# Feed-forward rows normalised inside the attention before it, and a projection that alternates between two banks

## The reference

```
x = x + tanh(g_xattn[0]) * window_attention(layernorm(x), ctx)      # 8 heads, window 16
x = x + tanh(g_ffn[0])   * quantised_ffn(layernorm(x))
x = x + tanh(g_xattn[1]) * lane_attention(layernorm(x), ctx, ctx)   # 4 lanes, mixed by a matrix
x = x + tanh(g_ffn[1])   * lora_swiglu(layernorm(x))

lora_swiglu(x): gate = x Wg' + (x Ag') Bg';  up = x Wu' + (x Au') Bu'
                h = silu(gate) * up;         out = h Wd' + (h Ad') Bd'
```

## Time and profile before

| what | value |
| --- | --- |
| median of 3 runs | 3566.77 us |
| all runs | 3562.18, 3566.77, 3567.2 us |
| the profiled execution | 3563.57 us, of which the span is 3561.9 us |
| PE busy in the span | 3269.9 us (92%) |
| DVE, ACT, POOL busy | 1429.4, 888.1, 348.5 us |
| blocks' first DMA at | w 0.80, f 413.39, kv 893.07, a 1333.90, l 1985.97, g 2004.87 us |

### The profile page before, as it was taken

How to read it: one execution, slowest core, us unless ns; L and a number is a source line. 1 busy time by engine, 2 the same in 40 slices (tenths; PEclk the granted TensorE clock), 3 DMA queues, 4 the chain that set the end, 5 groups by cost and what they waited for, 6 DMA issues and landing times. The chain is left out here.

```text
span 3561.9 us, 52640 instructions
## 1 busy us (share of the span) xinstructions
PE 3269.9 (92%) x21076; PEld 2512.2 (71%) x21076; DVE 1429.4 (40%) x2021; ACT 888.1 (25%) x1232; POOL 348.5 (10%) x304
## 2 busy tenths in 40 slices
PE   6999658998799996999999389999999999999999
PEld 3555545777688874666666378888888888778777
DVE  7787568882200006776776351122212211310000
ACT  2233243342211114554554121111111111200000
POOL 2000000000000002322322111111111110000000
PEclk9999779999699998999999699999999999999999
DMA  5666432221322213111211432222222222643443
GB/s 112 137 144 143 124 110 72 75 69 45 122 64 71 71 54 118 70 78 59 88 59 47 130 109 90 96 96 90 89 96 96 94 86 84 223 149 116 142 141 103
DMA packets 339441, 352.61 MB, mean 99 GB/s; under 512 B 154352, under 2 KB 261472, under 8 KB 337264
## 3 DMA queue, kind: packets, MB, share of 16 engines
q1 hardware_dynamic: 339312, 350.79, 31.6%
HBM read 215.23 MB, written 126.97 MB: 96 GB/s over the span
## 5 line engine op out<-in xcount | busy, mean ns | idle before, releaser
L2230 PE MATMUL g_ps<-g_xs,g_wt 128*128 128x512 f32 x4128 | 957.9, 392 | 0.0
L2230 PEld LDWEIGHTS g_ps<-g_xs,g_wt 128*128 128x128 f32 x4128 | 774.8, 189 | 160.8
L2286 PE MATMUL g_ps<-g_wd,g_h 128*128 128x512 f32 x2016 | 463.8, 392 | 6.4 <-DMA g_h<-g_hidden 3.3
L2286 PEld LDWEIGHTS g_ps<-g_wd,g_h 128*128 128x128 f32 x2016 | 380.9, 189 | 88.5 <-DMA g_h<-g_hidden 5.0
L2148 DVE SCALAR_TENSOR_TENSOR g_act_out<-g_ps,g_g,g_act_out 128x512 f32<-128x512 f32 (+1 forms) x88 | 66.0, 750 | 691.2 <-ACT g_act_out L2080 691.2
L2080 ACT ACTIVATE g_act_out<-g_ps 128x512 f32<-128x512 f32 (+1 forms) x88 | 52.6, 598 | 655.3 <-PE g_ps L2230 655.2
L1280 PE MATMUL kv_gps<-kv_xh,kv_wh 128*128 128x512 f32 x512 | 200.8, 392 | 0.0
L1280 PE MATMUL kv_gps<-kv_xl,kv_wh 128*128 128x512 f32 x512 | 199.4, 389 | 0.0
L1280 PE MATMUL kv_gps<-kv_xh,kv_wl 128*128 128x512 f32 x512 | 199.2, 389 | 0.0
L1025 PE MATMUL f_gps<-f_xt,f_qwh 128*128 128x256 f32 x1024 | 193.9, 290 | 1.4 <-DVE f_xt L903 1.4
L1628 PEld LDWEIGHTS a_tps<-a_ident,a_e 128*128 128x128 f32 x1024 | 112.1, 143 | 104.9 <-issue 91.2
(11 more groups left out here) (247 smaller groups left out, 4381.2 us busy)
## 6 DMA issues: line engine op xcount, KB each, us to landing
g_h<-g_hidden SPq DMA_DIRECT2D x176, 256.0 KB, 2.7
g_hidden<-g_h SPq DMA_DIRECT2D x84, 512.0 KB, 2.7
kv<-kv_y SPq DMA_DIRECT2D x16, 1024.0 KB, 5.7
a_kv<-kv SPq DMA_DIRECT2D x16, 1024.0 KB, 4.8
g_xb<-x SPq DMA_DIRECT2D x24, 512.0 KB, 4.1
g_down<-g_raw SPq DMA_DIRECT2D x22, 512.0 KB, 2.8
g_raw<-g_down SPq DMA_DIRECT2D x22, 512.0 KB, 4.1
g_raw<-in_L_ffn_gate_w_dram SPq DMA_DIRECT2D x21, 512.0 KB, 4.0
```

Source lines behind the costliest of these rows:

```text
L2230: w = pe.matmul(gps[:, c % 2, m, :], wt[m][i][:, l, ks], xs[c][:, r, k, :], start=(k == 0 and a == 0), stop=(k == NK - 1 and a == 2))
L2286: w = pe.matmul(to, tile[:, p % RING, l, cols], wd[f][:, r, os], start=(f == 0 and a == 0), stop=False)
```

## The change

- Window attention: the second half of the queries and of the values goes into the bank of the ring that the next batch's first or second scores will use (`half_bank`); x has five slots instead of four and is loaded one batch further ahead.
- `lora_stacks` is gone as a block. Its six loads and 18 stores stand on ACT's own DMA queue in `projections`, its two instructions on ACT and DVE there.
- Lane attention also normalises its finished rows: in event W, ahead of the addition of batch b-1, DVE and POOL normalise y of batch b-2 into `a_yn`, and SP stores it to `x3n`. The last batch is normalised after the last addition. The first pass of the loop is written out.
- Feed-forward loads these rows. Tiles 0 to 11 have eight slots `g_xa` in a part of memory that group 3 fills later; 12 to 15 use `g_xb`. Tiles 0 to 7 alternate between two pairs of banks. The first product waits for the gate's weights only, not for the up weights.

```diff
 window_attention
+        def half_bank(n, i, a):
+            return prj[:, :] if a == 0 or i == 1 else sps[:, (NK * n + i // 2) % RING, :]
 project
-                    pe.wait_ge(S["sbk"], 2 * n + 2) if a == 0 else pe.wait_ge(S["sbq"], 2 * n + 1)
+                    pe.wait_ge(S["sbk"], 2 * n + 2) if a == 0 else past(pe, "sel", NK * n - RING + 1)
 values
-                pe.wait_ge(S["sbq"], 2 * n + 2) if a == 0 else pe.wait_ge(S["sbv"], 2 * n + 1)
+                pe.wait_ge(S["sbq"], 2 * n + 1) if a == 0 else past(pe, "sel", NK * n - RING + 2)
 scores
+                if t == 1:
+                    pe.wait_ge(S["sbv"], 2 * n + 2)
...
 projections, ACT
+            for (a, _, _), at, width in zip(jobs, starts, widths):
+                act.dma_start(factors[:, at:at + width], flat(a)).then_inc(S["factors"], 16)
...
             weights(1, 1)
+            act.wait_ge(S["factors"], 16 * len(jobs))
+            act.copy(parts[:, 0, :], factors[:, :]).then_inc(S["high"], 1)
             results(0, 0)
+            act.wait_ge(S["low"], 1)
...
...
 lane_attention, POOL (end of a pass)
+                if not isinstance(b, int) or b >= 2:
+                    power(b - 2)
 lane_attention, DVE
+            def norm_rows(n):
+                layer_norm_steps(nc, dve, S, n, y, st, mv, S["rstd"])
+                dve.wait_ge(S["ynout"], 16 * n)
+                dve.tensor_scalar(yn[:, :], y[:, :], mv[:, 0:1], rstd[:, 0:1], ALU.subtract, ALU.mult).then_inc(S["yn"], 1)
                     elif ev == "W":
+                        if not isinstance(b, int) or b >= 2:
+                            norm_rows(b - 2)
+                            dve.wait_ge(S["yn"], b - 1)
                         result(b - 1, sl)
...
             result(B - 1, (LAST + 1) % 2)
+            dve.wait_ge(S["res"], B)
+            norm_rows(B - 1)
...
 swiglu_ffn
-        tps = ps[:, 6:8, :].rearrange("p a n -> p (a n)")
+        tps = [ps[:, i:i + 2, :].rearrange("p a n -> p (a n)") for i in (6, 2)]
+        def place(n):
+            if n < 12:
+                return xa[:, n % 8, :], xld[n % 8], 16 * (n // 8) + 16
+            return xb[n % 2][:, :], xld[8 + n % 2], 16 * (n // 14) + 16
+        def turned(n):
+            return tps[n % 2 if n < 8 else 0]
...
             def turn(n):
-                pe.wait_ge(S["xn"], n + 1)
-                if n:
-                    pe.wait_ge(S["xtl"], n)
+                src, done, value = place(n)
+                pe.wait_ge(done, value)
+                if n >= 2:
+                    pe.wait_ge(S["xtl"], n - 1 if n < 8 else n)
...
-                        pe.wait_ge(S["wl"], parts(f, 0) + 1 if is_last(f) else parts(f, 1) + 1)
+                        pe.wait_ge(S["wl"], parts(f, 0) + 1 if first or is_last(f) else parts(f, 1) + 1)
```

More of the change, by code:

```diff
@@ L110, in window_attention @@
         S = {n: s.sem(n) for n in names}
-        xl = [s.sem(f"xl{i}") for i in range(4)]
+        xl = [s.sem(f"xl{i}") for i in range(XS)]
         cl = [s.sem(f"cl{i}") for i in range(2)]
@@ L1059, with projections, flat @@
 TOK = B * P
-def projections(nc, tag, x_in, norm_x, w, bias, mixing, amp, out):
+def projections(nc, tag, x_in, norm_x, w, bias, mixing, amp, out, left, right, out_left, out_right):
+    jobs = [(a, o, (0, 1, 0)) for a, o in zip(left, out_left)] + [(a, o, (0, 0, 1)) for a, o in zip(right, out_right)]
+    widths = [a.shape[0] * a.shape[1] // P for a, _, _ in jobs]
+    starts = [sum(widths[:n]) for n in range(len(jobs))]
+    def flat(rows):
+        return rows.rearrange("r n -> (r n)").rearrange("(p c) -> p c", p=P)
     NB = w.shape[0] // P
@@ L1086, in projections @@
         bmix = s.sb("bmix", [P, NB])
+        factors = s.sb("factors", [P, sum(widths)])
+        parts = s.sb("parts", [P, 2, sum(widths)], F32R)
         st = s.sb("st", [P, 2, 6])
@@ L1097, in projections @@
         xld = [s.sem(f"xld{i}") for i in range(2)]
-        names = ("consts c1 am mt mg mix stats aggr rstd xn xt xth xtl wld wp wh wl bp bm g ge out").split()
+        names = ("consts c1 am mt mg mix stats aggr rstd xn xt xth xtl wld wp wh wl bp bm g ge out "
+                 "factors high low stacks").split()
         S = {n: s.sem(n) for n in names}
@@ L1238, in weights @@
                 dve.tensor_tensor(wl[i][:, :, :], wps[:, :, :], wh[i][:, :, :], ALU.subtract).then_inc(S["wl"], 1)
-            with dve.Fori(0, NB // 2) as j:
+            weights(0, 0)
+            weights(1, 1)
+            dve.wait_ge(S["high"], 1)
+            dve.tensor_tensor(parts[:, 1, :], factors[:, :], parts[:, 0, :], ALU.subtract).then_inc(S["low"], 1)
+            with dve.Fori(1, NB // 2) as j:
                 for i in range(2):
@@ L1479, in _ @@
             residual(B - 1)
+            power(B - 2)
+            power(B - 1)
         @block.scalar
@@ L1904, in _ @@
             sp.dma_start(g[:, 0:1], everywhere(gates[1:2], P)).then_inc(S["consts"], 16)
-            load_x(0)
-            load_x(1)
+            for n in range(4):
+                load_x(n)
             sp.wait_ge(S["zero"], 4)
@@ L1915, in _ @@
             load_factors(1, 1)
-            for n in range(2, 4):
+            for n in range(4, 14):
                 load_x(n)
@@ L1998, in _ @@
         def _(pool):
-            pool.memset(half[:, :], -0.5)
             pool.memset(la[:, :].bitcast(F32), 0.0).then_inc(S["zero"], 1)
@@ L2015, in low @@
                 pool.tensor_tensor(wt[m][i][:, 1, :], raw[m][:, :], wt[m][i][:, 0, :], ALU.subtract).then_inc(S["wl"], 1)
-            power(0)
-            power(1)
             low(0, 0, 0)
-            power(2)
             low(0, 0, 1)
-            for n in range(3, NT):
-                power(n)
             def step(f, i):
@@ L2253, in step @@
                     w = product(f, i, c, 0)
+                    if first and c == 0:
+                        pe.wait_ge(S["wl"], parts(f, 1) + 1)
                     if not is_last(f):
```

184 lines of the change are left out of this document (84 added, 100 removed).

## The result

| what | before | changed |
| --- | --- | --- |
| median of 4 runs, same chip | 3565.06 us | 3499.78 us |
| lowest to highest | 3562.18 to 3567.2 | 3498.44 to 3501.37 |
| the profiled execution, its span | 3563.57, 3561.9 us | 3501.37, 3499.6 us |

The account below looks back on a forecast made before the run. In window attention PE and DVE wait for each other; in lane attention only PE counts. Terms -16.5 -18.9 +1.5 +3.4 -13.2 -10.5 = -54.2 against 3563.57 gave 3509.4, predicted as 3510 us; own range 3496 to 3521, wide range 3494 to 3528.

Parts of the forecast that it names:

- Term 1: Window attention: separate banks for the halves and a fifth slot of x save 16.5 us, bounds 8 to 24.
- DVE's 19.5: Window attention: DVE's idle time in its chain between passes, 19.5 us together, taken as near the possible gain.
- late keys: Window attention: spread keys landing late for the next pass's first scores, for which 3 us came off the gain.
- The rival that keys hold this block: Window attention: keys or another chain replace the removed waits, leaving about 4 us saved, time 3522; chance 0.13.
- Term 2: Factor split moved into the projections: the removed block saves 18.9 us, 1.5 lost to memory at the start.
- the +1.5 behind it: Projections' start: factor loads beside the first context tiles delay PE's turns, 1.5 us lost, bounds 0 and 2.4.
- Term 3: Lane attention: normalising finished rows costs steady passes 0, and 3.4 us at the end for the last batch.
- The cover of 8.73: Lane attention: DVE idles 8.73 us for the output projection, hiding a 3.3 us normalising chain with 5.4 to spare.
- The rival that it outgrows its cover: Lane attention: normalising exceeds DVE's idle time, each us over costing PE one per batch; 3633, chance 0.02 for slower.
- Term 4: Feed-forward, start to fifth turn: turning tiles as they land, without normalising there, saves 13.2 us, bounds 8 to 17.
- the rival of memory: Feed-forward's start: bound by memory, factors and weights come late, 10 us lost, time 3520; chance 0.19.
- Term 5: Feed-forward's quarters with turns: group 0 saves 1.6 us, groups 1 and 2 save 8.9; together 10.5, bounds 5 to 14.

Follow-up runs that it names:

- e1: Kernel before with only the changed window attention (banks for the second halves and fifth slot of x): 3535.8 us, ratio 0.9915 to the kernel before.
- e11: Changed kernel with the six factor loads issued by ACT behind its context-tile copies and first weights instead of first: 3501.8 us.
- e10: Changed kernel with fourteen extra statistics on DVE in each batch's normalising chain of the lane attention: 3574.7 us.
- e7: Changed kernel with two pairs of banks for feed-forward groups 1 and 2 as well: 3497.3 us.
- e8: Changed kernel with the feed-forward's factors loaded behind two x tiles instead of four, and turn 1 ahead of the wait for them: 3503.3 us.
- e5: Changed kernel with one pair of banks for all sixteen turns of the feed-forward: 3503.9 us.
- e9: Changed kernel with six extra statistics on DVE in each batch's normalising chain of the lane attention: 3505.9 us.
- e6: Changed kernel with only two x tiles under way at the feed-forward's start, loaded as in the kernel before: 3510.7 us.

## Why the prediction was right

**Term 1, window attention, -16.5: right in kind, too small by 5.6.** Named rightly were the two waits that go, the fourth scores that want the first select as what is late next, and the pass (21.1 predicted, 21.03 measured). Mis-sized was the sum. DVE's 19.5 fits the first thirteen passes, which gained 21.1, but I took 3 off it for late keys, and PE doesn't wait for them. The gain ahead of the first result was left out: that result came at 77.2 and comes at 74.0, 3.2 earlier. Against it the last two passes took 2.1 longer, 39.5 for 37.4 us, with the clock at 0.87 from 344 to 368 us; that is this execution's, e1 took 35.2 for them. So 21.1 and 3.2 less 2.1 make the 22. One reading in the term is slightly off: the wait for values is not below 1 us a pass but 13.7 in 13, 1.05. The rival that keys hold this block falls with the same rows.

**Term 2, the split: -18.9 right, the +1.5 behind it wrong.** That two queues share the memory holds: the first turn is 1.3 us later with the loads ahead (6.4 in the mean of nine profiles, 5.1 of five), and e11 takes that back. The step that failed is "PE's turns are paced by loads after that, so a delay stays". No delay shows at the first product or in the length of the block, 441.0 us in the mean with the loads first and without; that it is made up for is shown within the spread of these profiles, how is open. The issues of the stores cost ACT 11.7 us and not 8; the cover, a block of 96 matmuls, held.

The Trainium skill (DMA: Bandwidth & Descriptors, section Queues, rings and completion order) has SP's and ACT's rings take turns on the engines. The runs agree as far as they go: the six factor loads landed 1.9 to 6.4 us after issue beside the tiles, and 1.9 to 2.7 in e11 without them, so the two queues do share; in what turns, no run shows.

**Term 3, lane attention: right.** The cover of 8.73 took a chain of 4.0, passes stay at 37.6, and the tail costs 3.1 for a forecast of 3.4. The rival that it outgrows its cover was priced by "each us costs PE one". e10 shows that the mechanism and its place were right, and that the price is higher. What made it unlikely, that POOL has only products of 1 us there, is borne out by 1.43 for the scaling.

**Term 4, start of the feed-forward: right for the reason given, and in part by luck.** 25.2 was forecast for the fifth turn, 24.6 measured. I had the factors there at 12 us after the first DMA; PE passed the wait for them at 11.5. Behind it two errors cancel: the turns and merges up to the fourth turn ended at 19.0 and not 21.7, since the clock rose in them, and what stands on DVE and ACT behind them took 5.6 and not 3.6. In e7, where the clock stayed low there, the fourth turn ended at 21.4 and the fifth began at 25.3, near the forecast's 21.7 and 25.2. Not foreseen was that 4.9 us of the wait for the factors are idle time of which a different order takes back 3.5 (e8). Against the rival of memory: no wait of PE for a tile stands behind the first, and none of DVE for weights.

**Term 5, the quarters: right in sum.** Group 0 took 16.9 for 16.4, groups 1 and 2 took 38.4 for 39. The waits of 2.84 were forecast as 2.8. The loss of clock was forecast for both and came behind turn 9 alone, 20.0 and 18.4 us for the two groups where 19.5 each was forecast; in e5, where it came behind both, they took 20.0 each. The part that I gave to the second pair of banks belongs to normalising (e5).

## What to carry to other kernels

Idle time on a helper engine can be spent at no cost to the bound engine as long as some of it remains (e9). One step further it can cost more than its own length, 1.8 times here (e10), because the matrix engine's clock can drop after the wait: measure what remains, not only what was used. Two edits that shorten the same loop should be tried together: here each alone gave 7 us in thirteen passes and both gave 21; with the banks alone more passes had to wait for a load. When a start is led by loads, look which load the first explicit wait names, and put that one ahead of the bulk.

## What the runs showed of the hardware

- In the lane attention two waits of 1.4 us each, 2.5 us apart, were followed by a granted clock of 0.50 for 3.4 and 6.8 us (e10), in passes that otherwise run at 1.00 throughout.
- The same wait can end either way. Turns 9 and 13 of the feed-forward wait 2.84 us each, and PE was busy at 1.00 for the 6 us before. In the changed kernel, e5, e6, e8, e9, e10 and e11 that makes 14 such waits; behind 8 of them the clock fell and the turn and its 12 products together took about 1.6 us longer (in the changed kernel 5.39 for 3.84), behind 6 it stayed. What decides between them no run shows.
- With the same code from there on, the steady part of the feed-forward read 1449 to 1458 us, and the last 45 us of the window attention differed by 4.3 (clock 0.87 or 1.00 from 344 to 368 us): one execution can't carry an edit of 5 us by its span, but milestones within it can.
- ACT paid 0.65 us for the issue of a store of a factor piece on average (11.7 for 18, and 0.44 to 1.09 in the mean of the three of one factor), where SP paid 0.47 for the same 18 stores in the kernel before.
